# Windowed attention's opening: row and context loads, statistics and projections given to later units, and one wait made narrower

## The chip, the cores and the metric

The kernel runs on one core of one Trainium2 chip. The metric is device time in microseconds (us) of one execution. Every time below comes from three timed executions or from one profiled execution of the kernel before.

## The reference

Two layers on 8 sequences of 256 tokens, 256 features wide: windowed attention of x on a context, a routed mixture of 16 experts with capacity, linear attention, a top-2 mixture of 8 experts. Only the first attention is touched:

```python
x = x + jnp.tanh(g_xattn[0]) * _L0_xattn_ref(_layernorm(x, axis=-1), ctx_1024, ctx_1024)
```

Query is the normalised x, key and value are the context, there are 16 heads of 16 features, and a key counts if it lies within 128 positions of the query. Linear attention, much later, needs the context times two 256 x 256 matrices (its keys and values); the kernel computes the first of these products early, between the units of the first attention.

## The kernel before

**Units.** The attention has 16 units: unit n is sequence n // 2 and half of the heads, n % 2. Its rows are the two row tiles (128 tokens each) of the sequence, so units 0 and 1 use x tiles 0 and 1, units 4 and 5 tiles 4 and 5, unit 8 tile 8. `over_units` (L85) gives each engine steps -2 to 18. Steps before LOOP_FROM are written out, then come LOOPS rounds of a loop with four steps in each, then the rest. Everything that is conditional on a fixed step number must stand in the steps written out.

**One step n.** Each engine has its own order, and semaphores join them:

- SyncE (L165 to L200) stores the transposed maxima of unit n-1 into row block KR:KM of `q6` (L177), writes the split parts of unit n+2 to the scratch tensor `scr` in three DMAs (L187), waits until they have landed, and reads them back, rearranged, into `q6` and `k6` in six DMAs (L198).
- GpSimd splits the maxima of unit n-1 into bf16 terms (L268 to L274), splits unit n+2's rows and context (L280 to L283), copies context for unit n+3 (L239), values for unit n (L289), and computes the power -1/2 of statistics (`rsqrt`, L246).
- ScalarE computes exponentials of unit n-2 (L327), copies unit n+2's transposed rows to bf16 (L347), copies the turned context tiles and their products (`keep_scalar`, L1447), then the transposed maxima of unit n-1 (L359), and last normalises the rows of unit n+3 (L315).
- VectorE takes the eight maxima of unit n (L423), three before and five behind the subtraction of line 435 that serves unit n+2, and adds results of unit n-3 to x (`norm`, L406 to L416). At a step's end it may compute `statistics` (L393 to L398) of a group of row tiles. These end in `shift` (L386), which waits for GpSimd's power. In steps -2 to 1 it then fills the rows KR:KM of one of the four slots of `k6` with ones (L447).
- TensorE does the first pass of unit n (L488, L490), the second pass of unit n-2 (L506, L508; unit m uses slot m % 4 of `k6`), the products with the values (L518), and transposes of unit n+2 (`split_transposes`, L470), which wait for the normalised rows. `lin.turn` (L1408) and `lin.multiply` (L1417) of the context tiles in PROJECT_AT stand between.

**Groups.** Rows and context come in five groups of tiles: 0-1, 2-3, 4-7, 8-11, 12-15. The first two x groups and the first three context groups are loaded ahead of the steps. Step 0 of SyncE starts with five loads of 512 KB each: context group 3, x groups 2, 3 and 4, context group 4. VectorE computes group 2's statistics at the end of step 0, group 3's in step 1, group 4's in step 2. GpSimd waits for all the context groups at the start of step 1 (L255). ScalarE waits at the end of step 1 for group 2's shift and at the end of step 2 for group 4's (L366). Before unit 0's second pass TensorE waits for all four slots of ones:

```python
if m.reg is None and m.c == 0:
    e.wait_ge(s_ones, 4)
```

Of the kernel before, what the change touches and what calls it, by code (L numbers as in the profile page):

```python
# [74 lines left out]
        e.wait_ge(sem, value)  # L75


LOOP_FROM, LOOPS = 3, 3
GROUPS = ((0, 2), (2, 4), (4, 8), (8, 12), (12, 16))
STATISTICS_AT = {-2: 1, 0: 2, 1: 3, 2: 4}  # L80
PROJECT_AT = {-2: (0, 2), -1: (2, 7), 0: (7, 9), 1: (9, 10)}
IN_START, IN_FIRST, IN_ROUTING, IN_GAP = 10, 11, 12, 14


# [11 lines left out]
def attention(nc, top, a, K):  # L96

    x_sb, ctx_sb, gates, identf = K["x"], K["ctx"], K["gates"], K["identf"]
    next_dve, next_pool, _, _ = K["ln_b"]
    x, ctx_in, g_x, g_f = a["x"], a["ctx_1024"], a["g_xattn"], a["g_ffn"]  # L100
    with ExitStack() as ctx:
# [30 lines left out]
        s_x = [sem(f"s_x{i}") for i in range(len(GROUPS))]  # L132
# [19 lines left out]
        @block.sync  # L152
        def _(e):
            def load(dst, src, i, s):
                t0, t1 = GROUPS[i]
                e.dma_start(dst[:, t0:t1, :], src.rearrange("b (c p) d -> p (b c) d", p=P)[:, t0:t1, :]).then_inc(s[i], 16)
            load(x_sb, x, 0, s_x)
            load(ctx_sb, ctx_in, 0, s_cx)
            e.dma_start(gates[:, 0:2], g_x.rearrange("(a n) -> a n", a=1).to_broadcast([P, 2])).then_inc(s_g, 16)
            e.dma_start(gates[:, 4:6], g_f.rearrange("(a n) -> a n", a=1).to_broadcast([P, 2])).then_inc(s_g, 16)  # L160
            load(ctx_sb, ctx_in, 1, s_cx)
            lin.load_kv(e)
            load(x_sb, x, 1, s_x)
            load(ctx_sb, ctx_in, 2, s_cx)

            def step(n):
                if n.reg is None and n.c == 0:
                    load(ctx_sb, ctx_in, 3, s_cx)
                    for i in range(2, len(GROUPS)):
                        load(x_sb, x, i, s_x)  # L170
                    load(ctx_sb, ctx_in, 4, s_cx)
                if n.reg is None and n.c == 2:
                    lin.load(e)
                m = n - 1
                if m.valid():
                    wait(e, s_mte, m.times(1, 1))
                    e.dma_start(q6[KR:KM, m.mod(4), :, :],  # L177
                                mts[:, m.mod(2), :, :].rearrange("p c t -> p (c t)")).then_inc(s_m[m.mod(4)], 16)
                u = n + 2
                if u.prepared():  # L180
                    r = u.mod(2)
                    wait(e, s_p3, u.times(2, 2))
                    if u.reg is not None or u.c >= 2:
                        v = u - 2
                        wait(e, s_q6[v.mod(4)], v.over4(96, 96))
                    for f in range(3):
                        e.dma_start(scr[r, f].rearrange("d h s t -> h d (s t)"),  # L187
                                    parts[:, r, 2 * f:2 * f + 2, :].rearrange("p s t -> p (s t)")).then_inc(s_scw[r], 16)
                if u.prepared():

                    wait(e, s_s2, (u - 4).times(4, 4))

                    cnt = 48 * (u.c // 2 + 1) if u.reg is None else u.reg * 96 + 48 * (u.c // 2 + 1)
                    wait(e, s_scw[r], cnt)
                    for r0, f0, nf in ((0, 0, 3), (3 * DH, 1, 2), (5 * DH, 2, 1)):
                        for s, dst in ((0, q6), (1, k6)):
                            ff = (0, 3 - f0) if s == 0 else (f0, 3)
                            e.dma_start(dst[r0:r0 + DH * nf, u.mod(4), :, :],  # L198
                                        scr[r, ff[0]:ff[1], :, :, s, :].rearrange("f d h t -> (f d) h t")
                                        ).then_inc(s_q6[u.mod(4)], 16)  # L200
            over_units(e, step, -2, NU)
            e.wait_ge(s_q6[NU % 4], 96 * (NU // 4 + 1))
            e.wait_ge(s_zr, 1)
            clear_rows(e, K["y0"], K)

        @block.gpsimd
        def _(e):
# [44 lines left out]
            def step(n):  # L252
                if n.reg is None and n.c == -1:
                    e.wait_ge(s_cx[1], 16)
                if n.reg is None and n.c == 1:  # L255
                    for i in range(2, len(GROUPS)):
                        e.wait_ge(s_cx[i], 16)
                first = n.reg is None and n.c < 0
                if first:
                    copy_ctx(n + 3)  # L260
# [47 lines left out]
        def _(e):  # L308
# [21 lines left out]
            def step(n):  # L330
                m, u = n - 2, n + 2
                first = n.reg is None and n.c < 0
                if first:
                    if n.c == -1:
                        e.wait_ge(s_nm, 2)
                    normalise(n + 3)
                if m.valid():
                    exps(m, 0)
                if (m - 1).valid():
                    evac(m - 1, 1)  # L340
                if u.prepared():
                    wait(e, s_tt, u.times(1, 1))
                    if u.reg is not None or u.c >= 2:
                        v = u - 2
                        cnt = 48 * (v.c // 2 + 1) if v.reg is None else v.reg * 96 + 48 * (v.c // 2 + 1)
                        wait(e, s_scw[u.mod(2)], cnt)
                    e.activation(parts[:, u.mod(2), 0:6:5, :], M[:].rearrange("p (s t) -> p s t", s=2),  # L347
                                 ACT.Copy).then_inc(s_p1, 1)
                if n.reg is None and n.c == 0:
                    normalise(n + 3)  # L350
                if n.reg is None and n.c in PROJECT_AT:
                    lin.keep_scalar(e, *PROJECT_AT[n.c], turned, product, lin.staged)
                if (n - 1).valid():
                    w = n - 1
                    wait(e, s_mt, w.times(1, 1))
                    if w.reg is not None or w.c >= 2:
                        v = w - 2
                        wait(e, s_m[v.mod(4)], v.over4(16, 16))
                    e.activation(mts[:, w.mod(2)], MT, ACT.Copy).then_inc(s_mte, 1)  # L359
                if m.valid():  # L360
                    exps(m, 1)
                if m.valid():
                    exps(m, 2)
                    evac(m, 0)
                    exps(m, 3)
                if n.reg is None and n.c in (1, 2):  # L366
                    e.wait_ge(s_nm, 2 * n.c + 1)
                if u.prepared() and not first and not (n.reg is None and n.c == 0):
                    normalise(n + 3)
            e.wait_ge(s_nm, 1)  # L370
# [88 lines left out]
        def _(e):  # L459
# [34 lines left out]
            def pass2(m, u):  # L494

                r = m.mod(4)
                if u == 0:
                    wait(e, s_m[r], m.over4(16, 16))
                    if m.reg is None and m.c == 0:
                        e.wait_ge(s_ones, 4)  # L500
                wait(e, s_e, m.times(4, u - 1))
                for a in range(2):
                    h = 2 * u + a
# [1762 lines left out]
```

## Time and profile before

| | us |
|---|---|
| median of 3 timed executions | 819.82 |
| lowest and highest | 812.01, 820.28 |
| the profiled execution | 823.78 |
| its span, first to last instruction | 822.1 |
| mean granted TensorE clock | 0.938 of full speed |

The profiled execution is longer than the median by 3.96 us. A row of a timeline gives the start, the time that the instructions took, the engine, the line, what is written and read, and in brackets how long the engine stood idle before and what ended that. SPq are DMA issues on SyncE; the transfer lands later. PEld is TensorE's weight load. In a row of windows the number before each "(x...)" is the busy time of an engine, PEclk is the granted clock of TensorE as a share of full speed, and the last two are the mean busy share of the DMA engines and the GB/s they moved.

### The profile page before, as it was taken

Reading aid. Unit: us, or ns where it says so; the run is one execution under the profiler, and the core shown is the slowest. Engines: PE = TensorE matmul, PEld = TensorE weight load, DVE = VectorE, ACT = ScalarE, POOL = GpSimd, SP = SyncE. Lnnn points to the kernel's source line nnn. Section 1 sums busy time; section 2 is a strip of 40 time slices with the busy share of each in tenths; the row PEclk is TensorE's granted clock in tenths of the full one; section 3 lists DMA queues with packets and bytes.
Section 4 is the critical chain, followed back from the end, with each engine's and each line's share of the span. In section 5 each row is a group of like instructions: output and inputs, shape, how many; then the busy total and the mean of one; then the engine's idle time right before and its main releaser. Section 6 shows DMA issues by size and latency. Waiting matters only on the chain. (4 is left out here: it accounts for less than half of the span.)

```text
span 822.1 us, 16518 instructions
## 1 busy us (share of the span) xinstructions
PE 729.4 (89%) x5290; PEld 609.1 (74%) x5295; DVE 372.4 (45%) x1091; ACT 319.9 (39%) x860; POOL 337.7 (41%) x453
## 2 busy tenths in 40 slices
PE   5778999998697999996888885799999999999994
PEld 2446666765485999995766662689999999999994
DVE  3467777776426744542877757212222112222111
ACT  3325666666504333331456531133322333323331
POOL 5232333332206465433346422535444555444432
PEclk9969999999859999998999767799999999999998
DMA  5864656665395699933234433546643443354311
GB/s 143 217 138 100 124 115 128 120 123 134 127 364 158 197 375 366 343 114 118 36 59 71 122 104 133 164 104 157 195 129 84 97 118 56 51 151 116 89 23 13
DMA packets 146833, 114.59 MB, mean 139 GB/s; under 512 B 50465, under 2 KB 138188, under 8 KB 146762
## 3 DMA queue, kind: packets, MB, share of 16 engines
q1 hardware_dynamic: 136490, 100.59, 45.0%
q0 software_dynamic: 10272, 13.13, 7.8%
q8 instruction: 36, 0.59, 0.3%
q14 instruction: 35, 0.29, 0.1%
HBM read 153.02 MB, written 24.40 MB: 216 GB/s over the span
## 5 line engine op out<-in xcount | busy, mean ns | idle before, releaser
L1021 ACT ACTIVATE e_hT<-e_HP,e_col 128x128 f32<-128x128 f32 x312 | 88.7, 369 | 186.7 <-PE e_HP L985 177.9
L985 PEld LDWEIGHTS e_HP<-e_rT,w_up 128*128 128x128 f32 x1248 | 147.2, 194 | 4.2 <-issue 1.5
L985 PE MATMUL e_HP<-e_rT,w_up 128*128 128x128 f32 x1248 | 147.9, 277 | 1.7 <-issue 1.3
L997 PE MATMUL e_Y<-w_down,e_hT 128*128 128x256 f32 x624 | 141.0, 379 | 0.0
L997 PEld LDWEIGHTS e_Y<-w_down,e_hT 128*128 128x128 f32 x624 | 115.6, 190 | 14.1
L1078 POOL DMA_INDIRECT out<-e_yo,d_table x39 | 63.1, 1618 | 129.2 <-DVE e_yo L1046 114.8
L1043 DVE TENSOR_TENSOR e_yo<-e_Y,e_b2b 128x256 f32<-128x256 f32 x39 | 16.5, 424 | 218.2 <-PE e_Y L997 218.2
L423 DVE TENSOR_REDUCE a_nm<-S 128x2 f32<-128x512 f32 x128 | 83.5, 683 | 43.9 <-PE S L490 43.0
L327 ACT ACTIVATE a_pexp<-S 128x1024 f32<-128x1024 f32 x64 | 64.7, 1016 | 32.2 <-PE S L508 31.9
L808 PEld LDWEIGHTS e_HP<-e_rT,w_up 128*128 128x128 f32 x512 | 61.2, 196 | 4.2 <-DVE e_rT L861 3.4
L808 PE MATMUL e_HP<-e_rT,w_up 128*128 128x128 f32 x512 | 61.6, 280 | 3.0 <-DVE e_rT L861 3.0
L488 PE MATMUL S<-a_k,a_q 96*128 96x256 bf16 x256 | 52.8, 282 | 9.2 <-DMA a_k<-scr 5.4
L849 ACT ACTIVATE e_hT<-e_HP,e_col 128x128 f32<-128x128 f32 x128 | 36.4, 368 | 58.4 <-PE e_HP L808 43.1
L820 PE MATMUL e_Y<-w_down,e_hT 128*128 128x256 f32 x256 | 57.7, 379 | 0.0
L506 PE MATMUL S<-a_q,a_k 99*128 99x256 bf16 x256 | 50.9, 276 | 4.8 <-DVE a_k L447 3.7
L820 PEld LDWEIGHTS e_Y<-w_down,e_hT 128*128 128x128 f32 x256 | 47.5, 190 | 5.8
L1066 POOL DMA_INDIRECT e_rows<-rows,d_table x39 | 40.4, 1037 | 20.5 <-issue 11.3
L1071 POOL DMA_INDIRECT e_gate<-gate,d_table x39 | 39.3, 1007 | 11.9 <-issue 11.9
L488 PEld LDWEIGHTS S<-a_k,a_q 96*128 96x128 bf16 x256 | 25.7, 100 | 24.6 <-DVE a_nm L423 17.1
L891 POOL DMA_INDIRECT y<-e_yo,b_table x16 | 16.7, 1045 | 56.9 <-DVE e_yo L868 56.4
L518 PE MATMUL O<-a_pexp,a_v 128*32 128x256 f32 x512 | 34.6, 388 | 5.2 <-DVE a_on L408 3.3
L280 POOL CAST a_parts<-a_res 128x512 bf16<-128x512 f32 x17 | 10.4, 610 | 69.8 <-DVE a_res L435 69.8
(326 smaller groups left out, 1236.0 us busy)
## 6 DMA issues: line engine op xcount, KB each, us to landing
w_up<-L_ffn_w_in SPq DMA_DIRECT2D x39, 1024.0 KB
w_down<-L_ffn_w_in SPq DMA_DIRECT2D x39, 1024.0 KB
w_up<-L_ffn_W_in SPq DMA_DIRECT2D x16, 1024.0 KB
w_down<-L_ffn_W_in SPq DMA_DIRECT2D x16, 1024.0 KB
e_b2b<-L_ffn_b_in SPq DMA_DIRECT2D x55, 128.0 KB
scr<-a_parts SPq DMA_DIRECT2D x51, 128.0 KB
a_q<-scr SPq DMA_DIRECT2D x17, 192.0 KB
a_k<-scr SPq DMA_DIRECT2D x17, 192.0 KB
```

What stands on the lines that cost most here:

```text
L327: e.activation(pexp[:, u].rearrange("p a b t -> p (a b t)"), S2[u % 2][:].rearrange("p a b t -> p (a b t)"), ACT.Exp).then_inc(s_e, 1)
L423: e.tensor_reduce(nm[:, n.mod(2), h, :], S1[h % 2][:], axis=AX.X, op=ALU.max, negate=True).then_inc(s_mx, 1)
L488: e.matmul(dst[:, c, :], q6[0:KR, r, h, P * c:P * c + P], k6[0:KR, r, h, :], start=True, stop=True)
L506: e.matmul(S2[u % 2][:, a, c, :], k6[0:KM, r, h, P * c:P * c + P], q6[0:KM, r, h, :], start=True, stop=True)
L808: i = e.matmul(HP[r][:, j, :], w1[:, n % WR, k, P * j:P * j + P], rT[:, r, k, :], start=(k == 0), stop=(k == 1))
L820: i = e.matmul(Y[r][:, 0:D], hT[:, r, j, :], w2[:, n % WR, j, :], start=(j == 0), stop=(j == NJ - 1))
L985: i = e.matmul(HP[r][:, j, :], w1[:, n % WR, k, P * j:P * j + P], rT[:, r, k, :], start=(k == 0), stop=(k == 1))
L997: i = e.matmul(Y[r][:, 0:D], hT[:, r, j, :], w2[:, n % WR, j, :], start=(j == 0), stop=(j == NJ - 1))
L1021: i = e.activation(hT[:, r, j, :], HP[r][:, j, :], ACT.Gelu, bias=col[:, n % 4, j:j + 1])
L1066: e.indirect_dma_start(rows[:, r], None, K["rows"], by(n, 0), bounds_check=TOK - 1, oob_is_err=False).then_inc(s_rw[r], 16)
L1071: e.indirect_dma_start(gate[:, n % 4], None, K["gate2"], by(n, 1), bounds_check=2 * TOK - 1, oob_is_err=False).then_inc(s_g[n % 4], 16)
L1078: e.indirect_dma_start(outs, by(n, 2), yo[:, n % YR], None, bounds_check=TOK - 1, oob_is_err=False, compute_op=ALU.add).then_inc(s_os[n % ...
```

## The change

Lines 78 to 81 and what reads them. The loop starts at step 7 and runs twice, so steps 3 to 6 are now written out. SyncE loads only context group 3 at the start of step 0; x groups 2, 3, context group 4 and x group 4 follow at the ends of steps 0, 1, 2 and 3, and the eight weight loads of `lin.load` move from step 2 to step 5. VectorE computes the statistics of groups 2, 3 and 4 at the ends of steps 1, 3 and 5. ScalarE and GpSimd wait for one group at a time, in steps 1, 5 and 6. Context tile 8 is projected in step 1 instead of step 0, together with tile 9. The second pass of unit m, for m under 4, waits until slot m has been filled.

```diff
-LOOP_FROM, LOOPS = 3, 3
+LOOP_FROM, LOOPS = 7, 2
-STATISTICS_AT = {-2: 1, 0: 2, 1: 3, 2: 4}
-PROJECT_AT = {-2: (0, 2), -1: (2, 7), 0: (7, 9), 1: (9, 10)}
+STATISTICS_AT = {-2: 1, 1: 2, 3: 3, 5: 4}
+PROJECT_AT = {-2: (0, 2), -1: (2, 7), 0: (7, 8), 1: (8, 10)}
+CONTEXT_AT = {1: 2, 5: 3, 6: 4}
+SHIFTED_AT = {1: 3, 5: 4, 6: 5}
+LOADS_AT = {0: ("x", 2), 1: ("x", 3), 2: ("ctx", 4), 3: ("x", 4)}
...
                 if n.reg is None and n.c == 0:
                     load(ctx_sb, ctx_in, 3, s_cx)
-                    for i in range(2, len(GROUPS)):
-                        load(x_sb, x, i, s_x)
-                    load(ctx_sb, ctx_in, 4, s_cx)
-                if n.reg is None and n.c == 2:
+                if n.reg is None and n.c == 5:
                     lin.load(e)
...
+                if n.reg is None and n.c in LOADS_AT:
+                    kind, i = LOADS_AT[n.c]
+                    load(*((x_sb, x, i, s_x) if kind == "x" else (ctx_sb, ctx_in, i, s_cx)))
...
-                if n.reg is None and n.c == 1:
-                    for i in range(2, len(GROUPS)):
-                        e.wait_ge(s_cx[i], 16)
+                if n.reg is None and n.c in CONTEXT_AT:
+                    e.wait_ge(s_cx[CONTEXT_AT[n.c]], 16)
...
-                if n.reg is None and n.c in (1, 2):
-                    e.wait_ge(s_nm, 2 * n.c + 1)
+                if n.reg is None and n.c in SHIFTED_AT:
+                    e.wait_ge(s_nm, SHIFTED_AT[n.c])
...
-                    if m.reg is None and m.c == 0:
-                        e.wait_ge(s_ones, 4)
+                    if m.reg is None and m.c < 4:
+                        e.wait_ge(s_ones, m.c + 1)
```

On SyncE, at the start of step 0, just behind the scratch reads of unit 1, there stood before:

```order
L156 DMA ctx_sb<-ctx_in 128x4x256
L156 DMA x_sb<-x_in 128x4x256 x3
L156 DMA ctx_sb<-ctx_in 128x4x256
L187 DMA scr<-a_parts 8x16x512 x3
L198 DMA a_q<-scr 48x8x256
```

In the kernel changed, in the same place (L159 is the load, L187 and L198 write and read the scratch, and the rows left out are four more reads of unit 2):

```order
L159 DMA ctx_sb<-ctx_in 128x4x256
L187 DMA scr<-a_parts 8x16x512 x3
L198 DMA a_q<-scr 48x8x256
L198 DMA a_k<-scr 48x8x256
...
L198 DMA a_k<-scr 16x8x256
L159 DMA x_sb<-x_in 128x4x256
L177 DMA a_q<-a_mts 3x8x256
L187 DMA scr<-a_parts 8x16x512 x3
```

The scratch writes and reads of unit 2 now stand ahead of the x load of group 2, and that load ahead of the maxima of unit 0.

On VectorE, from the subtraction in step 0 on, there stood before (rows of `stats`, `mv`, `vare` and `nmr` are the statistics):

```order
L435 TENSOR_TENSOR a_res<-M,a_parts 128x512
L423 TENSOR_REDUCE a_nm<-S 128x2 x5
L393 BN_STATS stats<-x_sb 128x6 x4
L396 BN_AGGR mv<-stats 128x2 x4
L398 TENSOR_SCALAR vare<-mv 128x4
L386 SCALAR_TENSOR_TENSOR nmr<-mv,rstd 128x4
L447 MEMSET a_k 3x1024
L423 TENSOR_REDUCE a_nm<-S 128x2 x3
```

and now, with each line number two higher:

```order
L437 TENSOR_TENSOR a_res<-M,a_parts 128x512
L425 TENSOR_REDUCE a_nm<-S 128x2 x5
L449 MEMSET a_k 3x1024
L425 TENSOR_REDUCE a_nm<-S 128x2 x3
L437 TENSOR_TENSOR a_res<-M,a_parts 128x512
L425 TENSOR_REDUCE a_nm<-S 128x2 x5
L395 BN_STATS stats<-x_sb 128x6 x4
L398 BN_AGGR mv<-stats 128x2 x4
L400 TENSOR_SCALAR vare<-mv 128x4
L388 SCALAR_TENSOR_TENSOR nmr<-mv,rstd 128x4
L449 MEMSET a_k 3x1024
```

The statistics behind unit 0's five reductions are gone, and those behind unit 1's are of group 2, where group 3's stood; the filling of slot 3 is still behind them.

## Rows read from the trace of the kernel before

**Rows 1.** The page's line of engines: busy time, share, instructions

```profile
PE 729.4 (89%) x5290; PEld 609.1 (74%) x5295; DVE 372.4 (45%) x1091; ACT 319.9 (39%) x860; POOL 337.7 (41%) x453
```

**Rows 2.** Windows, all engines: VectorE's marks of units 2 to 6, then 8 to 16

```profile
29.83:43.07 13.24, 8.33 (x49) 5.31 (x50) 8.69 (x22) 2.93 (x9) 4.42 (x10) 0.92 0.89 247
43.07:58.40 15.33, 10.46 (x54) 6.03 (x55) 8.68 (x21) 3.18 (x7) 4.37 (x10) 0.63 0.66 131
58.40:71.42 13.02, 10.10 (x105) 7.16 (x103) 8.58 (x24) 6.47 (x10) 4.43 (x10) 0.88 0.71 146
71.42:80.82 9.40, 9.40 (x112) 7.12 (x111) 7.38 (x16) 6.28 (x10) 3.46 (x9) 0.99 0.26 63
100.49:179.46 78.97, 73.12 (x851) 53.29 (x849) 59.63 (x122) 51.61 (x80) 28.05 (x72) 1.00 0.62 121
```

**Rows 3.** VectorE's timeline, steps 0 to 2

```profile
36.34 1.40 DVE L393 BATCH_NORM_STATS2 stats<-x_sb 128x6 f32<-128x256 f32 x4
...
39.48 0.16 DVE L386 SCALAR_TENSOR_TENSOR nmr<-mv,rstd 128x4 f32<-128x4 f32 x1 [1.13 <-POOL rstd L246]
...
53.77 0.91 DVE L447 MEMSET a_k<- 3x1024 f32 x1 [0.27 <-POOL a_mres L270]
...
58.40 0.68 DVE L435 TENSOR_TENSOR a_res<-M,a_parts 128x512 f32<-128x512 f32 x1
...
63.65 1.40 DVE L393 BATCH_NORM_STATS2 stats<-x_sb 128x6 f32<-128x256 f32 x4
```

**Rows 4.** TensorE's timeline, steps 0 to 2, and one row of the tail

```profile
34.34 0.41 PE L1408 MATMUL O<-identf,ctx_sb 128*128 128x128 f32 x2 [1.32 <-DMA ctx_sb<-ctx_in]
...
35.27 1.95 PE L1417 MATMUL S<-c_wkv,w_down 128*128 128x512 f32 x4
...
42.85 3.73 PE L1417 MATMUL S<-c_wkv,w_down 128*128 128x512 f32 x4
...
54.83 0.37 PE L506 MATMUL S<-a_q,a_k 99*128 99x256 bf16 x1 [3.73 <-DVE a_k L447]
...
194.23 0.28 PE L506 MATMUL S<-a_q,a_k 99*128 99x256 bf16 x1 [1.11 <-DMA a_q<-a_mts]
```

**Rows 5.** SyncE's DMA issues, steps -1 to 3, and one of the tail

```profile
25.56 0.59 SPq L198 DMA_DIRECT2D a_q<-scr  x1
...
29.45 0.59 SPq L156 DMA_DIRECT2D ctx_sb<-ctx_in  x1
...
33.12 2.80 SPq L187 DMA_DIRECT2D scr<-a_parts  x3
42.03 0.59 SPq L198 DMA_DIRECT2D a_q<-scr  x1
...
47.55 0.82 SPq L177 DMA_DIRECT2D a_q<-a_mts  x1
...
56.66 0.60 SPq L1375 DMA_DIRECT2D c_wq<-L_xattn_wq_in  x1
...
60.11 0.82 SPq L177 DMA_DIRECT2D a_q<-a_mts  x1
...
74.67 1.89 SPq L187 DMA_DIRECT2D scr<-a_parts  x3
79.09 0.61 SPq L198 DMA_DIRECT2D a_q<-scr  x1
...
191.18 0.80 SPq L177 DMA_DIRECT2D a_q<-a_mts  x1
```

**Rows 6.** Windows of half a microsecond, all engines: loads, then silence

```profile
39.00:39.50 0.50, 0.00 (x0) 0.00 (x0) 0.03 (x1) 0.26 (x1) 0.44 (x1) 1.00 1.08 338
...
41.50:42.00 0.50, 0.40 (x3) 0.34 (x4) 0.50 (x2) 0.00 (x0) 0.00 (x0) 0.50 0.04 14
```

**Rows 7.** ScalarE's timeline, end of step 1

```profile
47.16 0.36 ACT L359 ACTIVATE a_mts<-M 24x256 bf16<-24x256 bf16 x1
47.42 0.86 ACT L315 ACTIVATE a_qn<-x_sb,nmr,rstd 128x128 f32<-128x128 f32 x2
```

## The prediction, made before the changed kernel ran

> **What bounds the kernel now.** I read four views in this order. The page's line of engines shows TensorE busy for 89% of the span and VectorE for 45% [rows 1]; that is a mean over stages that have nothing in common, and the chain that ended last runs through the expert layers, so neither says what the attention's first units are worth. I therefore asked the windows between successive VectorE subtractions of line 435. There is one per step, in the middle of it, and it serves the unit two ahead, so they mark the pace: step 0 marks unit 2, step 6 marks unit 8. From mark to mark the opening takes 13.24, 15.33, 13.02 and 9.40 us, and in the settled loop eight units take 78.97 us, 9.87 us each [rows 2]. So steps 0 to 2 are 12.0 us longer than three settled steps. That is all that lies on the table, and part of it is work that only changes its place.
>
> Third, VectorE's timeline says what fills the extra: at the end of steps 0, 1 and 2 it computes the statistics of four row tiles. From 36.34 us to the end of the shift (39.48 + 0.16) that is 3.30 us, part of it a wait for GpSimd's power [rows 3]. Fourth, the timelines of TensorE, SyncE and ScalarE say who waits: TensorE idles 1.32 us for context tiles 8 to 11 and 3.73 us before the first second pass, for VectorE's filling of key slot 3, which stands behind the statistics [rows 4]; SyncE issues five loads, and the scratch reads behind them start at 42.03, 8.91 us after the scratch writes, against 4.42 us in the loop [rows 5]. The DMA engines still move 338 GB/s at 39.0 to 39.5, and almost nothing at 41.5, so the scratch writes stood behind the 2.6 MB of loads and had landed just before the reads [rows 6].
>
> **Step 0.** The loads of x groups 2 to 4 and context group 4 leave it, and so do the statistics of group 2 and the projection of tile 8. Without that tile's turn the 1.32 us wait goes. TensorE's next two products then follow as fast as VectorE takes them, and I book 1.0 us: unit 0's reductions end at 35.3 instead of 36.3. The statistics (3.30 us) go from this place. The mark of unit 3 came 43.07 - 39.64 = 3.43 us behind them, so it now comes at 35.3 + 3.4 = 38.7, 4.4 us earlier. The extra projection in step 1 starts behind the first two products and is not in front of it.
>
> **Step 1.** It now projects tiles 8 and 9. A projection is 1.95 us at the full clock and took 3.73 us at 42.85, where the granted clock was at the lower of its two levels (1.2 of 2.4 GHz; 0.63 as a mean over the window) after TensorE had stood idle [rows 2, 4]. With the stall gone I take the higher level. Five reductions at about 0.65 us and one projection between them bring VectorE to 43.5; the second projection ends at 44.4. ScalarE copies that product out before it copies the maxima of unit 0, as it did before: projection end 46.58, maxima copy at 47.16, SyncE's issue at 47.55, 0.97 us in all [rows 4, 5, 7]. The maxima thus leave at 45.4. In the tail, where nothing hid it, such a store issued at 191.18 released TensorE at 194.23, after 3.05 us [rows 4, 5]. So the first second pass can start at 48.4, against 54.83.
>
> The new wait for one filled slot costs nothing and by itself gains nothing. With four slots demanded, the first second pass could not start before slot 3 was filled behind the statistics; with one it can. But right behind it in TensorE's order stand the transposes of unit 4, which need the normalised rows of unit 4, and these now need group 2's statistics, which stand at this very place in VectorE's order. The wait is replaced, not removed. When are those statistics done? The scratch writes of unit 2 issue at 33.1 at the latest, the reads start 4.4 us later at 37.5, six of them take 3.9 us (25.56 to 29.45), and the x load issues at 41.4 [rows 5]. Its cost has no row of its own kind. The lower bound is 524 KB at 338 GB/s, 1.6 us, landing at 43.0; the upper is what context group 3 took with other traffic about it, 29.45 to 34.34, landing at 46.3 [rows 4 to 6]. The statistics then end at 46.8 (VectorE is busy until 43.5) to 49.6, ScalarE's two normalisations take 0.9 more (47.42 to 48.28) [rows 7], so the transposes can start at 47.7 to 50.5. The second pass ahead of them occupies 48.4 to about 49.4. I take the second pass; the other limit can add 1.1 us. From second pass to mark of unit 4 took 58.40 - 54.83 = 3.57 us [rows 3, 4], so the mark comes at 52.0: 6.4 us ahead.
>
> The Trainium skill ("DMA: Bandwidth & Descriptors", Queues, rings and completion order) says that each DMA engine consumes a ring's descriptors in order, and that a completion increment lands only after every earlier write of that engine. The trace agrees for step 0: full rate, then silence, then the reads. The rule also speaks against the change, since x group 2 now stands behind six reads: by it the load lands near the upper bound and the sum loses 1.1 us; if loads could pass reads, near the lower, and the maxima alone set the sum.
>
> **Step 2.** Its reductions end 5.25 us after the mark (58.40 to 63.65), at 57.3. No statistics follow, and from their old end (66.95) to the next mark, 71.42, it was 4.47 us. The mark of unit 5 comes at 61.7, 9.7 us ahead [rows 2, 3]. Unit 3's scratch writes follow the maxima's issue at 46.4, its reads 4.4 us later at 50.8, and six issues and the last landing bring them to about 57, just in time.
>
> **Steps 3 to 6.** The other two groups of statistics fall here, in steps 3 and 5. What one costs among both normalisations, exponentials and value products no row shows. The floor is 3.3 us less VectorE's idle time in a settled unit, (78.97 - 59.63) / 8 = 2.4, so 0.9; the ceiling is what step 1 exceeded a settled one by, 15.33 - 9.87 = 5.5 [rows 2]. I take 3.2, from step 2 (13.02 - 9.87), the nearest: the statistics stood in front of the same norm, for which TensorE's value products wait. Before, marks 5 to 8 took 29.1 us; now 3 x 9.87 + 2 x 3.2 = 36.0, so unit 8 is marked at 97.7 instead of 100.49: 2.8 us ahead. The weight loads at the start of step 5 hold SyncE for 3.4 us (56.66 to 60.11) in a queue that is nearly full; I cost them at nothing because the statistics of step 5 delay VectorE by as much, and 3.4 us once if that cover is missing. The other loads, one to a step, issue in 0.6 us and move in 1.6 us before the next scratch writes are ready. Four units more in straight code and four fewer in the loop: nothing seen at the loop's edges in the trace, zero to within 0.5 us. Everything after the attention starts when it ends, so the 2.8 us carry through.
>
> Sum: -9.7 at unit 5, +6.9 by unit 8, net -2.8 us. The profiled execution took 823.78 us (span 822.1), 4.0 us above the median of 819.82; applied to that median the forecast is 817.0 us. About 1% is what a measurement of this kernel can tell from no change: its three runs alone lie 8 us apart.
>
> **Rivals.** (A) The statistics hide. VectorE has 2.4 us idle per unit, and spread singly they may cost only 0.9 us each: gain 2.8 + 4.6 = 7.4, 812.4 us. For it: 59.63 busy of 78.97. Against it: that idle time is many short waits for TensorE, and step 2 with one group cost its full length. (B) The x rows land too late. Group 2 is read in the step in which it is issued. If it lands at 49.1 rather than by 46.3, everything from the mark of unit 4 shifts by 2.8 us and nothing is left: 819.8 us. For it: six reads of the scratch ahead of it, 3.9 us of issues. Against it: 338 GB/s for loads. (C) Slower, through the clock. TensorE now waits in steps 2, 3 and 5 for statistics, each wait about as long as the one after which it was granted the lower level; if each such step costs the 5.5 us of step 1 rather than 3.2, that is 4.6 us, and if tile 9's projection is again at the lower level another 1.8 us: 823.4 us. It decides from a mean granted clock under about 0.7 in steps 3 and 5. For it: 0.63 in step 1. Against it: step 2 kept 0.88 with the same statistics [rows 2].
>
> **Chances.** The forecast 0.55 (its own range 814 to 819), A 0.15, B 0.18, C 0.12. The range takes in most of A and all of B and nearly C, 810 to 823. Faster by over 1% (under 811.6) needs A with a favourable draw of runs, or the forecast with a very favourable one: 0.14. Slower by over 1% needs more than C: 0.09. Within 1%: 0.77.
>
> **What would show it.** Right: marks of units 3, 4 and 5 at about 38.7, 52 and 61.7; scratch reads of unit 2 from 37.5 at the latest; the first second pass at 48 to 49, released by the maxima's DMA, not by the slot filling; marks 5 to 6 and 7 to 8 about 13 us apart, 6 to 7 about 10. Wrong: a statistics step under 12 us (A), VectorE waiting for x rows beyond 47 (B), a granted clock of 0.7 or less in steps 3 or 5 (C), or TensorE waiting for scratch reads of unit 7 behind the weight loads, which I cost at nothing.

## The result, and the profile after

| | before | changed |
|---|---|---|
| first comparison, four executions each, median (lowest to highest), us | 819.26 (812.01 to 820.28) | 826.86 (821.26 to 831.02) |
| the profiled execution, us | 823.78 | 826.68 |
| its span, us | 822.1 | 825.0 |
| mean granted TensorE clock | 0.938 | 0.935 |

The ratio is 1.0084, 95% interval [1.0043, 1.0124]. The forecast was 817.0 us, with a range of 810 to 823. Ratios, and the medians given further down, leave out executions in a slower state that the chip shows now and then. Two later comparisons of the unaltered changed kernel, of twelve executions each, gave 1.0031 [0.9996, 1.0066] and 0.9994 [0.996, 1.0028]. Weighted by their intervals the three make 1.003, about 2.5 us slower. The first and the last lie further apart than their intervals allow, so sessions differ by more than an interval tells, and 1.003 can't be told from 1. What stands is that the gain that was forecast, a ratio of 0.9966, lies outside the first two intervals and at the lower end of the third.

The page's line of engines in the changed kernel, which answers to [rows 1]:

```profile
PE 732.6 (89%) x5295; PEld 609.5 (74%) x5295; DVE 372.7 (45%) x1091; ACT 320.6 (39%) x860; POOL 338.6 (41%) x453
```

It says nothing, as before. The windows between VectorE's marks (now the subtraction of L437) do. Changed kernel, marks of units 3 to 8, then 8 to 16; columns as in [rows 2]:

```profile
28.71:37.31 8.60, 6.53 (x43) 3.88 (x44) 6.67 (x12) 2.10 (x6) 3.42 (x9) 1.00 0.84 163
37.31:51.92 14.61, 9.88 (x57) 5.51 (x57) 8.78 (x21) 4.22 (x10) 4.39 (x10) 0.90 0.62 131
51.92:62.65 10.73, 10.73 (x111) 7.83 (x109) 6.56 (x14) 6.28 (x10) 3.43 (x9) 0.82 0.81 153
62.65:74.49 11.84, 9.37 (x109) 6.70 (x107) 9.26 (x26) 6.48 (x10) 4.53 (x10) 1.00 0.79 168
74.49:84.54 10.05, 9.14 (x109) 6.68 (x107) 7.29 (x17) 6.48 (x10) 3.52 (x9) 1.00 0.59 139
84.54:99.53 14.99, 11.52 (x104) 7.60 (x102) 9.26 (x26) 6.48 (x10) 4.53 (x10) 0.79 0.79 159
99.53:180.92 81.39, 74.86 (x854) 54.76 (x853) 59.71 (x122) 51.37 (x80) 27.99 (x72) 0.98 0.59 115
```

Unit 5 is marked at 62.65, 8.8 us ahead of before. The lead is lost behind that. One of the two statistics steps, from unit 5 to 6, takes 11.84 us, less than the 13.1 that the prediction allowed; but the other, from unit 7 to 8, takes 14.99, and the eight settled units take 81.39 instead of 78.97. TensorE's timeline of the changed kernel shows what ended its waits, in step 1, between the marks of units 7 and 8, and in a settled unit:

```profile
46.61 0.28 PE L508 MATMUL S<-a_q,a_k 99*128 99x256 bf16 x1 [1.59 <-DMA a_q<-a_mts]
...
49.46 0.69 PE L472 MATMUL M<-identf,a_qn 128*128 128x128 f32 x2 [2.00 <-ACT a_qn L317]
...
91.30 0.28 PE L490 MATMUL S<-a_k,a_q 96*128 96x256 bf16 x1 [1.51 <-DMA a_k<-scr]
...
93.88 0.40 PE L508 MATMUL S<-a_q,a_k 99*128 99x256 bf16 x1 [1.73 <-DMA a_q<-a_mts]
...
146.35 0.28 PE L490 MATMUL S<-a_k,a_q 96*128 96x256 bf16 x1 [2.00 <-DMA a_k<-scr]
```

and SyncE's issues in step 5 (eight weight loads, of which the first and the last are shown) say why the row at 93.88 waited:

```profile
87.23 0.60 SPq L1377 DMA_DIRECT2D c_wq<-L_xattn_wq_in  x1
...
90.38 0.25 SPq L1384 DMA_DIRECT2D c_row<-L_xattn_ln_beta_in  x1
90.67 0.81 SPq L177 DMA_DIRECT2D a_q<-a_mts  x1
91.60 1.87 SPq L187 DMA_DIRECT2D scr<-a_parts  x3
```

The store of the maxima leaves at 90.67, and 3.21 us later the second pass that needs it begins. That is the 3.05 us of the tail in [rows 4, 5] again. The matmul that took 0.28 us at 46.61 took 0.40 us at 93.88, on the lower clock. Two windows show the clock fall during this wait, to the lower of its two levels (1.2 of 2.4 GHz), after TensorE had stood idle twice, for 1.51 and 1.73 us:

```profile
86.00:93.20 7.20, 4.64 (x56) 3.21 (x53) 5.38 (x17) 4.14 (x7) 3.24 (x7) 1.00 1.08 190
93.30:99.50 6.20, 5.62 (x37) 3.52 (x38) 2.35 (x5) 2.01 (x3) 0.55 (x3) 0.50 0.49 122
```

The wait at 91.30 is another matter. It is for scratch reads that SyncE had issued from 83.32 on, ahead of the weight loads, and it stands in kernels without those loads too (e16 below).

The rest of the kernel, from the first load behind the attention (`b_wg`) to the end, is not touched by the change. Its windows in before, in the changed kernel, and in a later profile of the changed kernel:

```profile
215.51:822.10 606.59, 551.33 (x3524) 487.65 (x3529) 232.00 (x765) 203.17 (x659) 265.24 (x268) 0.93 0.51 143
```

```profile
217.21:825.00 607.79, 553.10 (x3529) 487.76 (x3529) 232.68 (x765) 203.60 (x659) 265.95 (x268) 0.93 0.50 142
```

```profile
215.85:810.40 594.55, 543.40 (x3524) 482.45 (x3529) 233.33 (x765) 203.44 (x659) 266.06 (x268) 0.94 0.52 146
```

The same code took 607.79 and 594.55 us, a difference five times what the change does in the attention. Most of it lies between sessions, and those whose chip is on record ran on different chips: 594.5 to 597.7 us in the first session of experiments, 603.1 to 606.2 in the second, 595.0 to 600.3 in the third, 594.4 to 597.8 in the fourth. Within one session it is still 3 to 5 us. So in every profile below I read the attention by itself: its marks, and the start of `b_wg` as its end.

### The profile page after: what moved, and what is told of

It is laid out like the page before. It is cut to its first block and busy times, and to the rows that moved or that the text cites. A ratio compares the mean times of both kernels' runs of the same rounds, so it can differ in the third digit from the quotient of the medians.

```text
span 825.0 us, 16261 instructions
## 1 busy us (share of the span) xinstructions
PE 732.6 (89%) x5295; PEld 609.5 (74%) x5295; DVE 372.7 (45%) x1091; ACT 320.6 (39%) x860; POOL 338.6 (41%) x453
## 5 line engine op out<-in xcount | busy, mean ns | idle before, releaser
L999 PE MATMUL e_Y<-w_down,e_hT 128*128 128x256 f32 x624 | 144.3, 384 | 2.6 <-issue 2.6
L822 PE MATMUL e_Y<-w_down,e_hT 128*128 128x256 f32 x256 | 57.7, 379 | 0.0
```

The source lines that it names most:

```text
L822: i = e.matmul(Y[r][:, 0:D], hT[:, r, j, :], w2[:, n % WR, j, :], start=(j == 0), stop=(j == NJ - 1))
L999: i = e.matmul(Y[r][:, 0:D], hT[:, r, j, :], w2[:, n % WR, j, :], start=(j == 0), stop=(j == NJ - 1))
```

## The experiments

Two suspects stood at the start. W: the eight weight loads in step 5 hold up the maxima and the reads. F: something about the loop that starts at 7. Sixteen runs followed the first comparison, in four sessions; five of them repeat a kernel (e5 and e13 the changed one, e9 the one before, e14 is e10 and e16 is e12). The attention of each profiled execution, in us, with the timed ratio to the kernel before in the same session:

| kernel | unit 5 marked | step to unit 8 | unit 8 marked | per settled unit | `b_wg` starts | ratio, interval |
|---|---|---|---|---|---|---|
| before | 71.42 | 9.76 | 100.49 | 9.87 | 215.51 | |
| before, again (e9) | 68.32 | 9.58 | 98.16 | 9.68 | 211.64 | 0.9985 [0.9957, 1.0013] |
| changed | 62.65 | 14.99 | 99.53 | 10.17 | 217.21 | 1.0084 [1.0043, 1.0124] |
| changed, again (e5) | 62.88 | 13.92 | 99.64 | 9.82 | 214.82 | 1.0031 [0.9996, 1.0066] |
| changed, again (e13) | 62.83 | 13.79 | 97.65 | 10.09 | 215.85 | 0.9994 [0.996, 1.0028] |
| e1 | 68.8 | 9.2 | 97.27 | 9.81 | 213.53 | 1.0038 [1.0008, 1.0068] |
| e2 | 67.72 | 9.5 | 96.18 | 9.95 | 213.13 | 1.0022 [0.9992, 1.0053] |
| e3 | 68.69 | 11.85 | 102.85 | 10.02 | 219.39 | 1.0038 [1.0004, 1.0071] |
| e4 | 65.11 | 13.4 | 100.4 | 10.03 | 217.05 | 1.0039 [1.0002, 1.0075] |
| e6 | 69.32 | 9.2 | 98.51 | 9.62 | 212.90 | 1.0013 [0.9974, 1.0052] |
| e7 | 63.05 | 12.57 | 98.06 | 9.94 | 219.17 | 1.0062 [1.0028, 1.0096] |
| e8 | 69.83 | 9.3 | 99.16 | 9.69 | 217.26 | 1.0066 [1.003, 1.0103] |
| e10 | 62.77 | 12.60 | 97.77 | 9.76 | 212.11 | 0.9986 [0.9957, 1.0015] |
| e11 | 69.80 | 9.7 | 98.98 | 9.74 | 214.48 | 1.0016 [0.9987, 1.0046] |
| e12 | 63.71 | 11.85 | 98.44 | 9.50 | 212.06 | 0.9962 [0.9932, 0.9992] |
| e14 (as e10) | 63.44 | 12.59 | 98.43 | 10.14 | 216.48 | 0.9982 [0.9951, 1.0013] |
| e15 | 62.84 | 14.65 | 100.94 | 9.52 | 214.06 | 0.9941 [0.9901, 0.998] |
| e16 (as e12) | 62.36 | 11.84 | 97.99 | 9.45 | 210.25 | 0.9954 [0.9915, 0.9993] |

**First session: one part at a time.** e1 is the kernel before with only the loop moved:

```diff
-LOOP_FROM, LOOPS = 3, 3
+LOOP_FROM, LOOPS = 7, 2
```

> The kernel before with steps 3 to 6 written out and two rounds of the loop instead of three, nothing else. Theory W (the weight loads in step 5 cost the time, by way of a late store of the maxima and TensorE's clock): the time of the kernel before, within 1.5 us (0.998 to 1.002), settled units at 9.9 us. Theory U (the written-out steps, or the other place of the loop's branch, make the settled units slower): 2 to 7 us slower, settled units at 10.1 us or more, with a unit of 13 us near step 11.

e2 is e1 with the second pass waiting for its own slot:

```diff
-                    if m.reg is None and m.c == 0:
-                        e.wait_ge(s_ones, 4)
+                    if m.reg is None and m.c < 4:
+                        e.wait_ge(s_ones, m.c + 1)
```

> As the first, and the second pass of unit m waits for slot m alone. Both theories: the same as the first run within 1 us or up to 3 us faster, since here the statistics of group 2 and the normalised rows of unit 4 are long done and TensorE's 3.7 us wait before the first second pass really goes; the statistics of group 3 still hold VectorE at that place, so that I expect 1 to 2 us at the mark of unit 4 (58.4 before) and nothing later.

e3 is the changed kernel with the weight loads back in step 2:

```diff
-                if n.reg is None and n.c == 5:
+                if n.reg is None and n.c == 2:
                     lin.load(e)
```

> The changed kernel with the eight weight loads back in step 2. Theory W: step 5 (mark of unit 7 to unit 8, 14.99 us) falls to 12 to 13 us, no wait of 1.7 us for the maxima there, and the time is 3 to 7 us below the changed kernel, near 818 to 822. In step 2 the loads must not cost more than 2 us. Theory U, and a theory S (the statistics in steps 3 and 5 cost it): within 2 us of the changed kernel, 0.5% or more slower than before.

e4 is e1 with only the statistics (and ScalarE's waits for them) spread out:

```diff
-STATISTICS_AT = {-2: 1, 0: 2, 1: 3, 2: 4}
+STATISTICS_AT = {-2: 1, 1: 2, 3: 3, 5: 4}
```

> The kernel before with the steps written out and the statistics of groups 2, 3, 4 at the ends of steps 1, 3, 5, as in the changed kernel; all loads, the wait for four slots and the projections as before. Theory S: slower than before by 3 us or more. Theory W: within 2 us of before, with step 5 at 12 to 13 us; the opening gains little, since step 0 keeps its loads and the scratch reads of unit 2 still start near 42.

All four came within 0.2% of each other, so at this size the total tells no parts apart; the marks do. The own-slot wait gains 1.8 us at the mark of unit 4 (54.41 in e2, 56.17 in e1) and, as the prediction said, hardly anything lasting by itself. With the weight loads in step 2 the step to unit 8 falls to 11.85 us, but step 2 takes 16.0 us, with a wait of 3.54 us for the maxima: the loads cost wherever SyncE must store maxima behind them. The statistics alone do not make the total longer than e1's (e4, 1.0039 and 1.0038), though e4's attention ends 3.5 us later in its profile. e1 fits neither theory whole: it has the ratio that U wanted and the settled units that W wanted.

**Second session.** e5 is the changed kernel unaltered. e6 is the kernel before with `LOOP_FROM, LOOPS = 11, 1`. e7 is the changed kernel with the weight loads at `n.c == 15`. e8 keeps the loop of before (`3, 3`) and its wait for all four slots, and spreads loads and statistics as far as the three written-out steps allow (statistics of groups 3 and 4 both in step 2, behind the filling of the slots), with the weight loads in step 15:

```diff
-STATISTICS_AT = {-2: 1, 0: 2, 1: 3, 2: 4}
-PROJECT_AT = {-2: (0, 2), -1: (2, 7), 0: (7, 9), 1: (9, 10)}
+STATISTICS_AT = {-2: (1,), 1: (2,), 2: (3, 4)}
+PROJECT_AT = {-2: (0, 2), -1: (2, 7), 0: (7, 8), 1: (8, 10)}
+LOADS_AT = {0: (("x", 2), ("ctx", 4)), 1: (("x", 3), ("x", 4))}
```

> The changed kernel once more, unaltered, beside the variants. Theory F (instruction fetches of 16 KB land in the scratch reads of the loop's first units and of the unit behind the loop's branch, a read then lands 0.5 to 1.1 us late, TensorE idles for two and is given the lower clock) and theory W for step 5: the marks come as in the first profile, unit 7 to 8 in about 15 us, unit 12 to 13 in 11 to 13 us. If the long units stand elsewhere, both are chance. Ratio to before 1.004 to 1.009.

> The kernel before with steps 3 to 10 written out and one round of the loop. Theory F: 16 KB fetches go on through units 8 to 16, their reads land 7.8 us or later after the first issue in several units, settled units at 9.9 to 10.3 us, 1 to 4 us slower than before. A theory L (the branch back to the loop's start itself costs it): there is no branch back any more, no unit above 10.6 us, and the time is that of the kernel before.

> The changed kernel with the eight weight loads in step 15, behind the loop, where nothing needs SyncE. Theory W: unit 7 to 8 falls from 15.0 to 12 to 13 us and no wait of over 1 us for the maxima stands there; 2 to 4 us faster than the changed kernel, about the time of before. Theory S (the statistics in a full step do it alone): 14.5 us or more as before.

> A version that keeps the loads apart and the projections, but stays with the loop from step 3: x group 2 and context group 4 at the end of step 0, x groups 3 and 4 at the end of step 1, statistics of group 2 at the end of step 1, of 3 and 4 together at the end of step 2 with one wait for GpSimd, slots filled ahead of them, weights in step 15. Theory F with W: no fetches beyond about 100 us, settled units at 9.8 to 9.9 us, mark of unit 8 at 95 to 97, 3 to 6 us faster than before. If the fetches do not matter, its gain is that of the opening alone and the settled units are at 10.0 or more, as in the changed kernel: within 1 us of before.

e5 repeated only part of what was expected: 13.92 us from unit 7 to 8, 10.54 from unit 12 to 13, where 11 to 13 had been expected, and a ratio of 1.0031. e8 was to gain 3 to 6 us and came out slower than before. e7 was a miss that taught something. Its step to unit 8 is 12.57 us, as W wants, but its attention ends later than any other but one. SyncE's issues in its tail, first and last of the weight loads and the store behind them:

```profile
189.12 0.43 SPq L1377 DMA_DIRECT2D c_wq<-L_xattn_wq_in  x1
...
193.65 0.25 SPq L1384 DMA_DIRECT2D c_row<-L_xattn_ln_beta_in  x1
193.94 0.84 SPq L177 DMA_DIRECT2D a_q<-a_mts  x1
```

and TensorE behind it:

```profile
196.25 0.39 PE L508 MATMUL S<-a_q,a_k 99*128 99x256 bf16 x1 [4.87 <-DMA a_q<-a_mts]
```

The wait that was 1.11 us in [rows 4] is 4.87 us. I had moved the loads to the one place where nothing hides them. e8 has the same wait (4.24 us at 195.21), which spoils it as a test of the loop. e6 broke F as I had put it: more straight code should have cost more, and its settled units are the fastest of its session.

**Third session: no load in front of any store.** e9 is the kernel before, unaltered, as a measure of the method. e10 is the changed kernel with the weight loads behind all units, e11 is e8 with the same edit, e12 is e10 with `LOOP_FROM, LOOPS = 11, 1`:

```diff
-                if n.reg is None and n.c == 5:
-                    lin.load(e)
...
             over_units(e, step, -2, NU)
+            lin.load(e)
```

> The kernel before itself, as if it were a variant: what the comparison and a second profile of it give where nothing differs. Ratio 0.997 to 1.003 with 1 inside its interval; unit 16's mark within 1.5 us of 179.5, no 16 KB instruction fetch between units 8 and 15. If the ratio lies at 1.003 or above, as for all seven variants so far, a part of their losses belongs to the comparison.

> The changed kernel with the eight weight loads behind all the units on SyncE. Theory W (the weights stood ahead of a store of maxima, for which TensorE waited 1.7 us in step 5 and 4.9 us in step 15): neither wait; unit 7 to 8 in 12 to 13 us; attention ends 2 us or more before the changed kernel's, 2 to 3 us faster than it. Rival: unit 7 to 8 stays near 14 and the time within 1 us of the changed kernel's; then it is the statistics.

> The version with the loop from step 3, statistics of groups 3 and 4 together in step 2, and the weights behind all the units. Theory W: unit 16's mark as in e8, 176.7, and the attention's end 4 us earlier than there, at 213 instead of 217.3: 2.5 us before that of the kernel before; 1 to 3 us faster than before. Rival R (what follows the attention takes up or gives back a few us by itself, through the clock): the end moves so and the total does not follow.

> The changed kernel with the weights behind all the units and steps 3 to 10 written out, one round of the loop. Settled units at 9.6 us as in e6 and no unit above 11 us behind unit 8; attention's end 3 to 5 us before that of the kernel before, total 2 to 5 us faster than before. Rival R as in e11: no gain in the total.

In e10 the store of unit 4's maxima leaves at 87.50, 3.2 us earlier than in the changed kernel. Its SyncE, its TensorE and its window from unit 7 to 8:

```profile
87.50 0.80 SPq L175 DMA_DIRECT2D a_q<-a_mts  x1
```

```profile
94.37 1.07 PE L519 MATMUL O<-a_pexp,a_v 128*32 128x256 f32 x16 [2.32 <-DVE a_on L409]
```

```profile
85.17:97.77 12.60, 9.96 (x105) 7.25 (x103) 9.26 (x27) 6.47 (x10) 4.53 (x10) 0.91 0.72 138
```

The wait for the maxima is gone, the one left is for the norm behind the statistics, and the step takes 12.60 us. The wait for the scratch reads is absent here too, but that isn't the loads' doing: e12 and e16, which have no weight load in step 5 either, show it at the same place. In e16:

```profile
92.58 0.28 PE L489 MATMUL S<-a_k,a_q 96*128 96x256 bf16 x1 [1.18 <-DMA a_k<-scr]
```

e12 was the first kernel below before with its whole interval. e11 was a miss: 1 to 3 us faster were expected, and the ratio is 1.0016, with the attention's end at 214.48 instead of 213.

e9 showed something about my own method. The windows of a second profile of the kernel before, marks of units 3 to 7 and 8 to 16:

```profile
29.19:43.32 14.13, 9.61 (x49) 5.52 (x50) 8.70 (x22) 2.93 (x9) 4.38 (x10) 0.88 0.94 245
43.32:56.44 13.12, 8.75 (x51) 5.50 (x51) 8.69 (x22) 3.18 (x7) 4.41 (x11) 0.75 0.57 117
56.44:68.32 11.88, 9.42 (x110) 6.88 (x109) 8.57 (x24) 6.47 (x10) 4.43 (x10) 0.99 0.75 148
68.32:78.18 9.86, 9.17 (x109) 6.65 (x107) 7.47 (x16) 6.48 (x10) 3.47 (x9) 1.00 0.61 117
98.16:175.60 77.44, 72.99 (x851) 53.32 (x849) 59.55 (x122) 51.57 (x80) 28.07 (x72) 1.00 0.62 123
```

Against [rows 2], steps 1 and 2 are 3.4 us shorter, with higher clocks (0.75 and 0.99 for 0.63 and 0.88), and step 0 is 0.9 us longer. The execution I had argued from was an unlucky one in just the steps that I counted as the gain; the expectation that unit 16 would be marked within 1.5 us of 179.5 failed (175.60). Its waits differ too. The 3.73 us wait for a filled slot, for which the narrower wait was made, isn't there. TensorE waits about as long for the scratch reads in its place, and in step 2, where the weight loads stood before the change, it waits for the maxima behind them:

```profile
51.41 0.37 PE L488 MATMUL S<-a_k,a_q 96*128 96x256 bf16 x1 [3.82 <-DMA a_k<-scr]
...
64.13 0.28 PE L506 MATMUL S<-a_q,a_k 99*128 99x256 bf16 x1 [1.76 <-DMA a_q<-a_mts]
```

So the kernel before already paid for the weight loads, in step 2.

**Fourth session: two by two.** W and F had so far been compared across sessions. e13 is the changed kernel, e14 has the weight loads behind the units, e15 has `LOOP_FROM, LOOPS = 11, 1` with the loads left in step 5, e16 has both.

> The changed kernel unaltered, as the corner of a two-by-two in one session. W and F both: 1.003 to 1.006 of the kernel before; step from unit 7's mark to unit 8's 14 to 15 us. If the changed kernel were really equal to before: 1.000 within 0.003.

> The changed kernel with the eight weight loads behind all units. W (they cost about 2.5 us in step 5): 0.3 to 0.5 per cent under e13, step from unit 7 to 8 12 to 13 us. Rival (they cost nothing, what remains is the loop): equal to e13 within 0.2 per cent.

> The changed kernel with LOOP_FROM, LOOPS = 11, 1, weight loads left in step 5. F (the loop from unit 7 with its branch back costs about 2.5 us): 0.3 per cent under e13, no unit of the settled part over 11 us. Rival W alone: equal to e13 within 0.2 per cent, the step from unit 7 to 8 still 14 to 15 us.

> Both edits. If W and F add: 0.6 to 0.8 per cent under e13 and 0.996 of the kernel before. If only W is real: as e14; if only F is real: as e15.

Medians: 813.90, 812.81, 810.39 and 807.87 us, against 813.34 before. The loop from 11 saves 3.5 us (e15 less e13) and 4.9 us (e16 less e14), and 3.0 us in the third session (e12, 808.90, less e10, 811.94). The ratios to before say the same, with less: 0.9947 for e15 to e13, 0.9972 for e16 to e14, 0.9976 for e12 to e10. Each alone is at the edge of its uncertainty of 0.4 to 0.5%, together they are 0.33% with an uncertainty of 0.27%. Without the loads in step 5 the medians fall by 1.1 and 2.5 us; the ratios of e14 to e13 and e16 to e15 are 0.9988 and 1.0013, so in total time that gain is not resolved. Of the expectations, the steps from unit 7 to 8 and e15's total held; that e14 would lie 0.3 to 0.5% under e13 and e16 0.6 to 0.8% did not (0.1 and 0.4% by the ratios). The windows of e13 and e16 show both in place, the step from unit 7 to 8 and the settled units:

```profile
83.86:97.65 13.79, 10.89 (x109) 7.37 (x107) 9.26 (x27) 6.48 (x10) 4.52 (x10) 0.88 0.75 160
97.65:178.40 80.75, 74.57 (x851) 53.98 (x849) 59.61 (x121) 51.67 (x80) 28.15 (x72) 0.98 0.62 119
```

```profile
86.15:97.99 11.84, 9.20 (x109) 6.76 (x107) 9.26 (x27) 6.47 (x10) 4.52 (x10) 1.00 0.72 136
97.99:173.60 75.61, 72.52 (x851) 53.36 (x849) 58.39 (x122) 51.16 (x80) 28.61 (x72) 1.00 0.63 124
```

e12, e15 and e16 are faster than the kernel before with their whole intervals, e15 by 0.59% and e16 by 0.46%, with the same work. The loop from 11 on the kernel before (e6) shows no such gain in total: 1.0013 [0.9974, 1.0052].

## Why the prediction was wrong, point by point

Two terms that the prediction put at nothing cost about 2 us each: the weight loads in step 5 and the loop's new place. And the gain itself was counted from a kernel before that is 1.2 us too late at unit 8. The terms in the order of the prediction:

**Steps 0 to 2: the marks were right, in part by luck.** Marks of units 3, 4 and 5: 38.7, 52.0 and 61.7 predicted, 37.31, 51.92 and 62.65 found. The first second pass starts at 46.61, not 48.4, released by the maxima's DMA and not by a filled slot. By the prediction's sum the mark of unit 4 should then have come at 50.2. It did not, because the limit that the prediction set aside was the one that counted: behind the second pass the transposes wait 2.00 us more, until 49.46, for the normalised rows. The wait for the slot was replaced, as said, but by one for the statistics, and these waited for the x rows of group 2. The changed kernel's VectorE:

```profile
45.18 1.41 DVE L395 BATCH_NORM_STATS2 stats<-x_sb 128x6 f32<-128x256 f32 x4 [2.87 <-DMA x_sb<-x_in]
```

The load was issued at 40.29, behind the six scratch reads, of which the last had landed at 43.93, and its rows released VectorE 4.89 us after the issue. That is what the prediction's upper bound allowed (29.45 to 34.34), only the issue came 1.1 us earlier than the 41.4 taken. The Trainium skill's page "DMA: Bandwidth & Descriptors" (Queues, rings and completion order) puts the completion increment behind every earlier write of the same DMA engine; the trace agrees with that in so far as the rows came 1.25 us behind the last read. No run issued this load ahead of the reads, so it isn't shown that the order made it late. Rival B's landing at 49.1 did not come, but its mechanism, a mark that waits for x rows, did. Step 2 was mis-sized: 9.7 us predicted, 10.73 found, at a clock of 0.82 (10.8 on average in the three profiles of the changed kernel).

**"-9.7 at unit 5": the term was mis-sized, by its base.** The mark of unit 5 was right within about 1 us; what it was subtracted from was not. Before marks unit 5 at 71.42 in one profile and 68.32 in the other, and unit 8 at 100.49 and 98.16. On average the lead at unit 5 was 7.1 us. Against the second profile, my own 97.7 would have been a gain of 0.5 us, not 2.8. The prediction took each duration from a single execution in which TensorE stood at 0.63 and 0.88 in these steps, and corrected only its total to the median.

**Statistics, "I take 3.2": about right, but not in the changed kernel.** Its step from unit 5 to 6 takes 11.84 us in all three profiles, 2.1 more than the 9.74 of a settled unit with the loop of before. Six other runs have the same steps up to that place (e7, e10, e12, e14, e15, e16), and there this step takes 13.21 to 14.04 us, with a lower clock (0.77 to 0.88). The nine make 13.0 us on average, 3.3 more than a settled unit. Rival A's 0.9 is out. Why the step is shorter in the changed kernel stays open.

**Weight loads, "I cost them at nothing because the statistics of step 5 delay VectorE by as much": failed.** With loads and statistics both in step 5, that step took 14.99, 13.92, 13.79 and 14.65 us (changed three times, e15), 14.3 on average; with the statistics but without the loads 11.85, 13.4, 12.57, 12.60, 11.85, 12.59 and 11.84 (e3, e4, e7, e10, e12, e14, e16), 12.4. So they cost 2.0 us in that step; no value of the one group lies inside the other. The cover is not there because the two delays stand in different chains: the statistics delay the norm and the value products, the loads delay the maxima's store and so the second pass, which comes earlier in TensorE's order. In all four profiles with the loads TensorE waits 1.70 to 2.50 us for the maxima there; in the seven without them it does not wait for them at all in that step. The lower clock behind that wait (0.50 in the window from 93.30) makes the rest slower. The price that I had named if the cover was missing, 3.4 us, was too high. The sign of being wrong that I had named, TensorE waiting for the scratch reads of unit 7, did not appear either: in the changed kernel no wait for them stands between 99 and 112 us. The loads hurt by the maxima of unit 4.

At the mark of unit 8 less is left of it: 99.44 on average with the loads (changed three times, e15), 98.14 without (e7, e10, e12, e14, e16), 1.3 us. And in the changed kernel the cost is hidden in the sum, since marks 5 to 8 took 36.15 us on average where 36.0 had been predicted: the cheap statistics of step 3 paid for the loads. That term of the sum was right by luck.

**"Four units more in straight code ... zero to within 0.5 us": failed.** A settled unit took 9.68 to 9.87 us with the loop from 3 (before twice, e8, e11; mean 9.74), 9.76 to 10.17 with the loop from 7 (ten profiles; mean 9.97), and 9.45 to 9.62 with the loop from 11 (e6, e12, e15, e16; mean 9.52). Over eight units the changed kernel's loop costs 1.8 us and the loop from 11 gains 1.8. In the changed kernel itself it was 10.03 against 9.775 before (three and two profiles), 2.0 us. My first explanation, that straight code costs, had the wrong sign: the loop from 11 has the most of it.

**The sum.** The forecast was 2.8 us ahead at unit 8, carried to the end. Of that, 1.2 were never there, because before marks unit 8 at 99.3 on average and not at 100.49, and 1.1 went in steps 0 to 2 (unit 5 marked at 62.8 on average, not 61.7). That leaves 0.4 ahead at unit 8 (98.9 in three profiles against 99.3 in two). Then 2.0 were lost in the settled units, where nothing had been expected, and 0.7 in the tail: 2.4 us later at `b_wg` (213.6 on average before, 216.0 changed). The direction agrees with 1.003 of the total, but the two profiles of before lie 3.9 us apart there, so 2.4 is no measurement by itself. The first comparison's 7.6 us are not accounted for: in the two profiled executions 1.7 us of the difference arise up to `b_wg` and 1.2 behind it, and the others have no trace.

**Rival C** had the right sign by the wrong way. It decided at a clock under 0.7 in steps 3 and 5 for waits for statistics; these were at 1.00 and 0.79, and the clock of step 5 fell during the wait for the maxima. e10, with only the wait for the norm there, still had 0.91.

**What stays open.** Why the loop from 7 is slower than both others. In half of its ten profiles one settled unit is over 12 us: 13.0 in the changed kernel, 12.7 in e3, e4 and e13 (unit 12 to 13 in all four), 12.9 in e14 (unit 11 to 12). e2 and e7 have units of 11.0 to 11.4; no unit is over 10.6 in the other three, nor in any profile with the loop from 3 or from 11. In the five long ones the last of a unit's six scratch reads landed 8.27 to 8.59 us after the first was issued, a fetch of 16 KB of instructions had begun 5.4 to 5.8 us after that issue, TensorE waited 1.75 to 2.00 us for the reads, and the granted clock then was at its lower level for 3.4 us. e2 and e7 have reads of 7.9 to 8.4 us and waits of 1.5 to 2.0 us, without the low clock. In the changed kernel the scratch reads issued from 137.64 released TensorE only at 146.35, 8.7 us later (the row in the section on the result), and VectorE waited in turn:

```profile
151.46 0.69 DVE L425 TENSOR_REDUCE a_nm<-S 128x2 f32<-128x512 f32 x1 [3.18 <-PE S L492]
```

What makes the reads late is likely the fetching of instructions (last section), but no run took the fetches away and left the rest, so it isn't shown. The DMA queues of e13's settled units, then e16's (queue, packets, MB, share); q8 has no row there in e9:

```profile
q1 hardware_dynamic: 16481, 9.51, 61.1%
q8 instruction: 4, 0.07, 0.5%
```

```profile
q1 hardware_dynamic: 15957, 9.26, 62.3%
q8 instruction: 7, 0.11, 0.7%
```

e16 fetches more and is the fastest, so fetches are no steady cost. The loop from 7 is the only one that fetches and also branches back in these units; that this is the cause is a guess, no run took the two apart, and e14's long unit lies a unit ahead of the place of the others.

## What to carry to other kernels

- Two delays cover each other only if they end at the same wait. A batch of small loads put into a nearly full DMA-issuing queue costs at the first latency-bound store behind it: here 3.4 us of issues cost 2.0 us in the step concerned, and in the tail, where they took 4.8 us, TensorE's wait grew by 3.8 us. Put it behind the last such store.
- Before a gain of a few us is claimed from windows of one profile, look at the granted clock of those windows, and at a second profile: what is "on the table" at 0.63 may be gone in the next execution, and so may the wait that the change is for (3.73 us in one profile of the kernel before, none in the other).
- When a sum takes the later of two limits, check afterwards which of them ended the wait. Here the mark was right and the limit was the other one.
- Moving a loop's edge is a change of its own: here 1.8 us lost or gained over eight units against the loop of before, 3.0 to 4.9 us of the total between the two new places. Try it alone, with several sizes.

## What the runs showed of the hardware that was not expected

- Where a fetch of 16 KB of instructions (one packet of 0.9 to 1.9 us) falls into a unit's scratch reads, they tend to land late. In all eighteen profiles, units 2 to 16, the last of the six reads landed 7.39 us after the first was issued when no fetch began between (172 units, 5 of them at 7.8 or more, none above 7.93), and 7.79 us when one began 3 to 6 us after that issue (66 units, 30 at 7.8 or more). All 15 groups of reads that took 8.2 us or more had a fetch 5.3 to 5.8 us after their first issue. That is an association: the window was chosen after looking, and no run was made for it.
- One SyncE issue in a batch can take far longer than its neighbours: 1.96 us for the fourth weight load in e7's tail, between issues of 0.47 and 0.30 us.
- Identical code behind the attention took 594.4 to 607.8 us in the profiled executions, of which 3 to 5 us arose within one session.
- The kernel before was profiled twice, with a granted clock of 0.63 and 0.75 in step 1, and the step took 15.33 and 13.12 us.
